# Thirty-one matrix products without a reader, placed on TensorE ahead of the first transposes and ahead of the first projection of a four-layer perceiver block

## The chip, the cores and the metric

The kernel runs on one core of one Trainium2 chip. The metric is device time in microseconds (us) of that core. Beside the times there is one profiled execution, from which all rows below are taken; its time axis begins at the first instruction. TensorE is called PE in the rows (PEld is its weight load), VectorE DVE, ScalarE ACT, GpSimd POOL, and SPq is the queue from which the loads are issued.

## What is computed

Two sequences of 256 tokens with 256 features go through a layer normalisation and then four layers of self-attention, cross-attention over a context with a lookback mask, and a gated feed-forward part. After that come one windowed attention layer and one feed-forward layer with quantised weights. Only the very beginning matters here:

```python
x = x + _L0_xattn_ref(_layernorm(x, axis=-1), ctx_1024, itok_BxS_0_255, ...)
# in _L0_xattn_ref, four times:
h = rmsnorm(x, n1[l])
qkv = h @ Wqkv[l].T + bqkv[l]
q, k, v = jnp.split(qkv, 3, axis=-1)
q = apply_rope(split_heads(q, H), cos, sin)
k = apply_rope(split_heads(k, H), cos, sin)
```

## The kernel before

The program is written engine by engine: each engine has its own list of calls, in an order written out by hand, and counted semaphores tie the lists together. A token block b (0 or 1) has 256 tokens in two tiles of 128. An engine carries out its list strictly in order, so an instruction that waits holds up everything behind it on that engine.

The start of the program is one chain through four engines. SyncE's queue issues the loads one after the other: the input `X0` of both blocks, then `const` (an identity matrix, causal mask, rotary tables), then the norm weights, the first weights, and the rest. VectorE takes the mean and variance of block 0, GpSimd makes the inverse roots (`lrs`, `rstd`), and VectorE writes the normalised rows `hs`. TensorE turns them with four transposes against the identity in `const` (`norm_T(0, 0, 0)`, line 320). VectorE copies the result out of PSUM and weights it, into `hT` (line 1744, `weigh_T`). TensorE then projects them to queries and keys (`queries_keys(0, 0, 0)` and `(0, 0, 1)`, line 326: for each token tile two products of 128x128 weights by 512 columns, in float32). VectorE adds the bias on the way out of PSUM (`HID`, line 1752, `biased_qk`), and rotates (`AQ`, lines 1770 to 1791), and TensorE transposes the rotated rows (`rotated_T`, line 359), and so on.

On VectorE the copy to `hT` of block 0 stands ahead of the second half of block 1's normalisation (`X`, line 1936, and `hs`, line 1735), and that stands ahead of the first `HID`.

TensorE writes small results to four PSUM banks in turn. A dictionary `uses` numbers the uses in the order in which TensorE's list makes them. Use n writes bank n modulo 4 and waits until the use four before it was emptied; `filled` and `emptied` give the other engines the count to wait for:

```python
def next_bank(l, use):
    uses[l, use] = len(uses)
def bank(l, use):
    return psD[uses[l, use] % DBANKS]
def free_for(l, use):
    return free(l, use), uses[l, use] // DBANKS + 1
```

VectorE counts all four banks as free once before its first work. `pool_set` is counted by GpSimd when it has written `ones`, a 128x128 float32 tile. TensorE's list begins with a wait for `c_ld`, the landing of `const`.

Of the kernel before, what the change touches and what calls it, by code (L numbers as in the profile page):

```python
# [14 lines left out]
P = 128  # L15
# [62 lines left out]
def perceiver(nc, x_in, ctx_in, seg_in, wa_in, wb_in, wc_in, nrm_in, bias_in, vec_in, wt_in, wf_in, const_in, out):  # L78
    stack = ExitStack()
    with stack:  # L80
        def sb(name, shape, dt=F32):
            return stack.enter_context(nc.sbuf_tensor(name, shape, dt))
# [4 lines left out]
        def sem(name):  # L87
            return stack.enter_context(nc.semaphore(name))
# [83 lines left out]
        ones = sb("ones", [P, P])  # L172
# [48 lines left out]
        pool_set, tern_step = sem("pool_set"), sem("tern_step")  # L221
# [27 lines left out]
# [6 lines that stand above are left out]
        def full(l, use):  # L255
            return d_full[uses[l, use] % DBANKS]

        def free(l, use):
            return d_free[uses[l, use] % DBANKS]
# [4 lines left out]
        def free_for(l, use):  # L264

            return free(l, use), uses[l, use] // DBANKS + 1

        def emptied(l, use):
            return free(l, use), uses[l, use] // DBANKS + 2
# [43 lines left out]
        def _(pe):  # L313
            def transposes(l, use, src):

                next_bank(l, use)
                pe.wait_ge(*free_for(l, use))
                for k in range(KT):
                    for t in range(QT):
                        mm = pe.transpose(bank(l, use)[:, k * L + t * P:k * L + (t + 1) * P],  # L320
                                          src[:, t, k * P:(k + 1) * P], ident)
                mm.then_inc(full(l, use), 1)

            def project(l, use, col, lhs, rhs, n=D):
                for k in range(KT):
                    mm = pe.matmul(bank(l, use)[:, col:col + n], lhs(k), rhs(k), start=(k == 0), stop=(k == KT - 1))  # L326
                return mm

            def norm_T(l, i, b):
                pe.wait_ge(h_set[b], l * NORMS + i + 1)  # L330
                transposes(l, f"n{i}{b}", hs[:, 2 * b:2 * b + 2, :])

            def queries_keys(l, b, t):
                pe.wait_ge(*emptied(l, f"n0{b}"))
                pe.wait_ge(wa_ld, l * 16 + 16)
                use = f"qk{b}{t}"
                next_bank(l, use)
                pe.wait_ge(*free_for(l, use))
                project(l, use, 0, lambda k: hT[b][:, k, t * P:(t + 1) * P], lambda k: Wqkv[:, k, 0:2 * D], 2 * D)\
                    .then_inc(full(l, use), 1)  # L340
# [400 lines left out]
            def quantised_down(t):  # L741
# [6 lines left out]
                                   WQ[2][:, f * D:(f + 1) * D], start=(f == 0), stop=(f == FT - 1))  # L748
                mm.then_inc(full(NL, f"d{t}"), 1)

            def sums():

                next_bank(NL, "sum")
                pe.wait_ge(asum_set, 3 * ABS_CHUNKS)
                pe.wait_ge(pool_set, 1)
                pe.wait_ge(*free_for(NL, "sum"))
                pe.matmul(bank(NL, "sum")[:, 0:3 * ABS_CHUNKS], ones[:, :], asum[:, :], start=True, stop=True)\
                  .then_inc(full(NL, "sum"), 1)
# [119 lines left out]
                pv(l + 1, 2)  # L878
            pe.wait_ge(c_ld, 16)

            norm_T(0, 0, 0)
            queries_keys(0, 0, 0)
            queries_keys(0, 0, 1)
            norm_T(0, 0, 1)
# [73 lines left out]
            def rest(further):  # L958
# [137 lines left out]
                if further:  # L1096
                    all_blocks(NL - 1, 1)
                sums()
                gate_up(NL - 1, 0, 5)
                out_T(NL - 1, 1, "coT1", 9)  # L1100
# [1659 lines left out]
```

## Time and profile before

| | |
|---|---|
| three timed runs | 622.4, 620.0, 622.28 us (median 622.28) |
| profiled execution, its own time | 619.67 us |
| span of that execution in the trace | 617.9 us |
| TensorE busy (product spans) | 564.1 us, 91% of the span |
| VectorE busy | 353.5 us, 57% |
| mean granted TensorE clock in the records | 0.991 |

The profiled execution's time is 1.8 us more than its span, for what lies around the first and last instruction. A busy TensorE in these rows is not TensorE at its peak: the spans of products overlap, since the next one begins before the last has left the array. A float32 product stands in the records as two weight loads and two passes, a transpose as one of each.

### The profile page before, as it was taken

The numbers are of one execution on the slowest core, as the hardware profiler recorded it, in microseconds if no ns is written. First come the engines' busy times: TensorE is split into PE (matmuls) and PEld (weight loads), VectorE is DVE, ScalarE is ACT, GpSimd is POOL, SyncE is SP. The second block draws the span as 40 slices with busy tenths as digits, with TensorE's granted clock in tenths as the row PEclk, the third lists the DMA queues.
The fourth block names the chain that finished last, engine by engine and source line by source line (L and its number), as shares of the span: only waits on it lengthen the run. The fifth ranks groups of instructions, "written<-read, shape, count | busy, mean of one in ns | idle before, by whom it ended". The sixth has DMA issues, their size and how long they took to land.

```text
span 617.9 us, 13676 instructions
## 1 busy us (share of the span) xinstructions
PE 564.1 (91%) x5806; PEld 421.8 (68%) x5806; DVE 353.5 (57%) x680; ACT 279.5 (45%) x490; POOL 117.7 (19%) x124
## 2 busy tenths in 40 slices
PE   4989998999999899999998989999898989999855
PEld 1666655988767566988766658987666558897523
DVE  5896445466564454674554455574554364752787
ACT  0254444633355336433544446342554547445523
POOL 4252100012323100020612000122312001252110
PEclk9999999999999999999999999999999999999969
DMA  8800020010500200201400200204000200000001
GB/s 334 345 2 25 12 69 2 5 65 1 205 2 4 102 1 3 68 1 27 180 1 36 70 2 2 69 1 189 16 2 1 71 0 2 0 1 2 2 1 39
DMA packets 4676, 30.29 MB, mean 49 GB/s; under 512 B 1153, under 2 KB 1665, under 8 KB 2818
## 3 DMA queue, kind: packets, MB, share of 16 engines
q1 hardware_dynamic: 4610, 29.35, 12.5%
q8 instruction: 49, 0.80, 0.5%
q14 instruction: 17, 0.14, 0.1%
HBM read 28.82 MB, written 0.52 MB: 47 GB/s over the span
## 4 chain that ended last, share of the span: by engine, by line
PE 77%; DVE 10%; ACT 8%; issue 3%; POOL 1%; DMA 1%; SPq 0%; DVEq 0%; POOLq 0%
PE psD L326 18%; PE QD L621 12%; PE psD L634 9%; PE QD L408 6%; PE QD L443 4%; ACT PTR L1253 3%; PE psD L320 3%; PE QD L436 3%; PE QD L394 3%; DVE AQ L1803 3%; PE psD L463 2%; PE QD L431 2%; PE psD L359 2%; PE psD L484 2%; PE psD L470 2%
## 5 line engine op out<-in xcount | busy, mean ns | idle before, releaser
L1253 ACT ACTIVATE PTR<-QD 128x2048 f32<-128x2048 f32 x40 | 75.1, 1878 | 41.8 <-PE QD L443 21.5
L326 PE MATMUL psD<-WAB,hT 128*128 128x256 f32 (+1 forms) x216 | 70.1, 465 | 2.2 <-DVE hT L1744 2.2
L2492 POOL TENSOR_TENSOR rstd<-ms,mhalf 128x2 f32<-128x2 f32 x26 | 19.9, 764 | 271.8 <-DVE ms L1729 270.6
L1803 DVE TENSOR_REDUCE AQ<-QD 128x8 f32<-128x2048 f32 (+1 forms) x24 | 55.0, 2290 | 27.0 <-PE QD L408 27.0
L621 PE MATMUL QD<-HH,WFH 128*128 128x256 f32 x224 | 67.4, 301 | 0.4 <-DVE WFL L1903 0.4
L1903 DVE TENSOR_TENSOR WFL<-WC,WFH 128x512 fp32r<-128x512 f32 x64 | 48.0, 755 | 32.2 <-ACT WFH L1297 32.1
L621 PE MATMUL QD<-HL,WFH 128*128 128x256 f32 x224 | 63.3, 283 | 0.0
L621 PE MATMUL QD<-HH,WFL 128*128 128x256 f32 x224 | 63.3, 283 | 0.0
L1800 DVE TENSOR_REDUCE AQ<-QD 128x16 f32<-128x2048 f32 x16 | 36.7, 2293 | 39.9 <-PE QD L408 39.9
L634 PE MATMUL psD<-WC,HID 128*128 128x256 f32 x256 | 58.2, 380 | 0.0
L326 PEld LDWEIGHTS psD<-WAB,hT 128*128 128x128 f32 x216 | 39.7, 195 | 21.0 <-issue 14.2
L1297 ACT ACTIVATE WFH<-WC 128x512 fp32r<-128x512 f32 x64 | 40.2, 629 | 26.0 <-PE QD L621 25.4
L634 PEld LDWEIGHTS psD<-WC,HID 128*128 128x128 f32 x256 | 47.4, 190 | 6.8 <-issue 1.0
L2534 POOL TENSOR_SCALAR_AFFINE_SELECT PTR<-PTR 128x1024 f32<-128x1024 f32 (+1 forms) x24 | 34.4, 1434 | 90.4 <-ACT PTR L1253 90.4
L408 PE MATMUL QD<-AQ 32*128 32x128 f32 (+1 forms) x1024 | 46.5, 312 | 0.0
L1261 ACT ACTIVATE QO<-psD 128x512 f32<-128x512 f32 (+1 forms) x40 | 20.5, 511 | 56.2 <-PE psD L470 40.6
L1222 ACT ACTIVATE hs<-X 128x256 f32<-128x256 f32 x48 | 19.5, 408 | 57.2 <-DVE X L1833 57.2
L621 PEld LDWEIGHTS QD<-HH,WFH 128*128 128x128 f32 x224 | 42.8, 191 | 3.2 <-issue 2.0
L408 PEld LDWEIGHTS QD<-AQ 32*128 32x128 f32 x1024 | 35.1, 185 | 13.9 <-issue 13.5
L621 PEld LDWEIGHTS QD<-HH,WFL 128*128 128x128 f32 x224 | 42.9, 191 | 0.9 <-issue 0.7
L621 PEld LDWEIGHTS QD<-HL,WFH 128*128 128x128 f32 x224 | 42.8, 191 | 0.0
L1833 DVE TENSOR_TENSOR X<-X,psD 128x512 f32<-128x512 f32 x24 | 16.5, 688 | 40.3 <-PE psD L326 29.5
(172 smaller groups left out, 1021.2 us busy)
## 6 DMA issues: line engine op xcount, KB each, us to landing
WC<-in_wc SPq DMA_DIRECT2D x4, 3072.0 KB, 10.9
WAB<-in_wa SPq DMA_DIRECT2D x4, 1024.0 KB, 4.9
WAB<-in_wb SPq DMA_DIRECT2D x4, 1024.0 KB, 4.7
WF<-in_wf SPq DMA_DIRECT2D x1, 3072.0 KB, 22.8
bias<-in_bias SPq DMA_DIRECT2D x4, 512.0 KB, 3.4
WAB<-in_wt SPq DMA_DIRECT2D x1, 1024.0 KB, 6.0
X<-in_x SPq DMA_DIRECT2D x2, 256.0 KB, 2.8
out_x<-X SPq DMA_DIRECT2D x4, 128.0 KB, 2.4
```

Source lines behind the costliest of these rows:

```text
L326: mm = pe.matmul(bank(l, use)[:, col:col + n], lhs(k), rhs(k), start=(k == 0), stop=(k == KT - 1))
L408: mm = pe.matmul(quad[a][:, at:at + keys], QKT[b][rows(a), s, q * P:(q + 1) * P], QKT[b][rows(a), s, L:L + keys], start=False, stop=True, ...
L443: mm = pe.matmul(quad[a][:, at:at + P], QKT[b][rows(a), s, L + k * P:L + (k + 1) * P], Q2[rows(a), n * P:(n + 1) * P], start=(at == 0), st ...
L621: mm = pe.matmul(S[:, w * L:(w + 1) * L], wp[:, m, :], hp[:, k, :], start=(k == 0 and j == 0), stop=(k == KT - 1 and j == 2))
L634: mm = pe.matmul(bank(l, use)[:, t * D:(t + 1) * D], AT[b][:, f, t * P:(t + 1) * P], Wd[:, f, :], start=(f == 0 and t == 0), stop=(f == FT ...
L1253: nc.scalar.activation(PTR[:, r % 2, :], QD[:, :], ACT.Exp, scale=SCALE).then_inc(t_exp, 1)
L1261: nc.scalar.activation(OA[:, 0:n], bank(l, use)[:, 0:n], ACT.Copy).then_inc(free(l, use), 1)
L1297: nc.scalar.activation(w_high(n), WCt[:, :, f * P:(f + 1) * P], ACT.Copy).then_inc(wh_set, 1)
L1800: v = dve.tensor_reduce(QKR[b][:, :, 0, h, MAXROW].rearrange("p t (s r) -> p r s t", r=SG_H), QD[:, :].rearrange("p (r s t n) -> p r s t n ...
L1803: v = dve.tensor_reduce(QKR[b][:, t, 0, h, MAXROW].rearrange("p (s r) -> p r s", r=SG_H), QD[:, :].rearrange("p (r s n) -> p r s n", r=4, ...
L1903: dve.tensor_tensor(w_low(n), WCt[:, :, f * P:(f + 1) * P], w_high(n), ALU.subtract).then_inc(wl_set, 1)
L2534: nc.gpsimd.affine_select(T, T, [[0, 16 // (t + 1)], [1, P]], ALU.is_ge, 0.0, base=0, channel_multiplier=-1)\
```

## The change

A new function `unread_products` takes a PSUM bank for itself, writes n products of `ones` by `ones` (128x128 by 128 columns, float32) to it, and counts the bank as filled after the first and as emptied after the last. It stands on TensorE's list at two places: 27 products behind the wait for `const` and a new wait for `pool_set`, ahead of `norm_T(0, 0, 0)`; and 4 products behind these transposes, ahead of `queries_keys(0, 0, 0)`. Since `uses` numbers all uses, every later small result moves to another of the four banks, on all engines alike.

```diff
+            def unread_products(use, n):
+
+                next_bank(0, use)
+                pe.wait_ge(*free_for(0, use))
+                for i in range(n):
+                    mm = pe.matmul(bank(0, use)[:, 0:P], ones[:, :], ones[:, :], start=True, stop=True)
+                    if i == 0:
+                        mm.then_inc(full(0, use), 1)
+                mm.then_inc(free(0, use), 1)
...
             pe.wait_ge(c_ld, 16)
 
+            pe.wait_ge(pool_set, 1)
+            unread_products("idle0", 27)
             norm_T(0, 0, 0)
+            unread_products("idle1", 4)
             queries_keys(0, 0, 0)
             queries_keys(0, 0, 1)
             norm_T(0, 0, 1)
```

This is TensorE's list of instructions at the start of the program, with + where the changed kernel has a row that the kernel before has not, and - for the reverse (L756 are the new products, L320 the transposes of `hs`, L326 the projections, each row with its number of products; float32 products count once here).

```order
 L312 UNCONDITIONAL_BRANCH
-L320 MATMUL psD<-const,hs 128x128 x4
+L756 MATMUL psD<-ones 128x128 x27
+L320 MATMUL psD<-const,hs 128x128 x4
+L756 MATMUL psD<-ones 128x128 x4
 L326 MATMUL psD<-WAB,hT 128x512 x4
 L320 MATMUL psD<-const,hs 128x128 x4
```

Nothing else moved: the transposes are the same four, now behind 27 products, and the first projection is behind 4 more.

The next rows are the head of the same list in the changed kernel, with the semaphores that each row waits for.

```order
0 L312 UNCONDITIONAL_BRANCH [waits barrier_Pool_Activation_PE_DVE_SP_release]
1 L756 MATMUL psD<-ones 128x128 [waits d_free0,pool_set,c_ld]
2 L756 MATMUL psD<-ones 128x128 x26
3 L320 MATMUL psD<-const,hs 128x128 [waits d_free1,h_set0]
4 L320 MATMUL psD<-const,hs 128x128 x3
5 L756 MATMUL psD<-ones 128x128 [waits d_free2]
6 L756 MATMUL psD<-ones 128x128 x3
7 L326 MATMUL psD<-WAB,hT 128x512 [waits d_free3,wa_ld,d_free1]
```

The wait for `const` (`c_ld`), which stood on the first transpose, is now on the first of the 27 products; the transposes wait for `hs` (`h_set0`) and the projection for `hT` (`d_free1`) as before.

## Rows read from the trace of the kernel before

**Rows 1.** The page: busy time and share; busy tenths in 40 slices.
```profile
PE 564.1 (91%) x5806; PEld 421.8 (68%) x5806; DVE 353.5 (57%) x680; ACT 279.5 (45%) x490; POOL 117.7 (19%) x124
PEclk9999999999999999999999999999999999999969
```

**Rows 2.** Waits of PE, 0 to 30 us: in total, times, longest (us).
```profile
PE psD L320 <- DVE hs L1735: 8.1, 1, 8.1
PE psD L326 <- DVE hT L1744: 1.0, 1, 1.0
```

**Rows 3.** Timeline, all engines, to 8 us: start, busy us, instruction, idle before.
```profile
0.95 0.20 POOL L2487 MEMSET ones<- 128x128 f32 x1
...
5.74 0.20 ACT L1308 ACTIVATE warm<-mhalf 128x1 f32<-128x1 f32 x1 [3.22 <-DMA const<-in_const]
5.78 0.72 POOL L2497 TENSOR_TENSOR lrs<-lve,mhalf 128x2 f32<-128x2 f32 x1 [1.70 <-DMA const<-in_const]
...
7.42 0.62 DVE L1735 TENSOR_SCALAR hs<-X,rstd 128x256 f32<-128x256 f32 x2
```

**Rows 4.** Timeline of PE, 8 to 24 us.
```profile
8.13 1.08 PE L320 MATMUL psD<-const,hs 128*128 128x128 f32 x4 [8.13 <-DVE hs L1735]
10.26 6.66 PE L326 MATMUL psD<-WAB,hT 128*128 128x512 f32 x8 [1.04 <-DVE hT L1744]
16.75 0.60 PE L320 MATMUL psD<-const,hs 128*128 128x128 f32 x4
17.36 1.09 PE L359 MATMUL psD<-const,AQ 128*128 128x128 f32 x8
...
20.19 1.17 PE L408 MATMUL QD<-AQ 32*128 32x128 f32 x32
...
21.79 1.88 PE L326 MATMUL psD<-WAB,hT 128*128 128x512 f32 x4
```

**Rows 5.** Timeline of PEld, 12 to 17 us: the weight loads of the passes.
```profile
12.13 0.34 PEld L326 LDWEIGHTS psD<-WAB,hT 128*128 128x128 f32 x1 [0.52 <-issue]
12.98 0.34 PEld L326 LDWEIGHTS psD<-WAB,hT 128*128 128x128 f32 x1 [0.52 <-issue]
...
15.54 0.34 PEld L326 LDWEIGHTS psD<-WAB,hT 128*128 128x128 f32 x1 [0.52 <-issue]
16.33 0.14 PEld L320 LDWEIGHTS psD<-const,hs 128*128 128x128 f32 x1 [0.45 <-issue]
```

**Rows 6.** Weight loads by form: busy us, mean ns of one.
```profile
L634 PEld LDWEIGHTS psD<-WC,HID 128*128 128x128 f32 x256 | 47.4, 190 | 6.8 <-issue 1.0
```

**Rows 7.** Timeline of DVE, 9 to 24 us.
```profile
9.33 0.88 DVE L1744 TENSOR_SCALAR hT<-psD,nrm 128x256 f32<-128x256 f32 x2
...
11.65 0.61 DVE L1735 TENSOR_SCALAR hs<-X,rstd 128x256 f32<-128x256 f32 x2
14.15 0.69 DVE L1752 TENSOR_TENSOR HID<-psD,bias 128x512 f32<-128x512 f32 x1 [1.89 <-PE psD L326]
...
16.61 0.69 DVE L1791 TENSOR_TENSOR AQ<-AQ,HID 128x512 f32<-128x512 f32 x1 [0.17 <-DVE HID L1780]
...
23.78 0.69 DVE L1752 TENSOR_TENSOR HID<-psD,bias 128x512 f32<-128x512 f32 x1
```

**Rows 8.** Windows near the end: busy us of each engine, then granted clock.
```profile
602.00:603.00 1.00, 1.00 (x3) 0.25 (x2) 0.61 (x1) 0.49 (x1) 0.00 (x0) 0.50 0.00 0
603.00:604.00 1.00, 1.00 (x5) 0.34 (x3) 0.64 (x1) 1.00 (x2) 0.00 (x0) 0.83 0.00 0
```

**Rows 9.** Timeline of PE near the end.
```profile
599.70 5.58 PE L728 MATMUL QD<-WAB,QO 128*128 128x512 bf16 x16 [0.68 <-issue]
```

**Rows 10.** Windows, 20 to 50 us: busy us of PE, PEld, DVE, ACT, POOL.
```profile
20.00:25.00 5.00, 5.00 (x58) 3.43 (x60) 4.15 (x5) 0.60 (x1) 0.45 (x1) 1.00 1.08 461
...
30.00:40.00 10.00, 8.98 (x140) 6.50 (x142) 9.60 (x18) 5.56 (x7) 4.90 (x4) 1.00 0.00 0
40.00:50.00 10.00, 9.04 (x161) 6.27 (x157) 9.22 (x20) 3.46 (x5) 3.04 (x3) 1.00 0.01 3
```

**Rows 11.** The chain of work that ended last, at its start: start, us, what.
```profile
1.73 3.99 DMA const<-in_const
5.78 0.72 POOL lrs L2497
...
10.26 6.66 PE psD L326 x8
16.92 0.44 PE psD L320 x4
17.36 0.67 PE psD L359 x4
```

## The prediction, made before the changed kernel ran

> **What bounds the kernel now.** I read the page first: TensorE is busy for 91% of the span [rows 1], so time given to it can only be free where it waits. Then the waits of TensorE in the first 30 us: it waits 8.1 us for the first rows `hs` and 1.0 us for `hT` [rows 2]. These two holes are the ones that the 31 products are put into. The question is when the products can start, how long they last, and whether they buy a faster clock.
>
> The timeline says when the holes are open. GpSimd has written `ones` at 0.95 + 0.20 = 1.15 us, but `const` has only landed when ScalarE and GpSimd, both waiting for it, go on at 5.74 and 5.78 us [rows 3]. TensorE's first instruction waits for `const` in both kernels. So the first hole is usable from about 5.75 us, not from 1.15, and it closes when `hs` is written: 7.42 + 0.62 = 8.04 us [rows 3], with the first transpose at 8.13 [rows 4]. That is 2.3 us of cover.
>
> The same rows show two speeds of TensorE. Passes of 512 columns follow each other by 12.98 - 12.13 = 0.85 us from 12 us on [rows 5], while the same form takes 1.88 / 4 = 0.47 us each at 21.79 [rows 4]. Four transposes took 1.08 us at 8.13 and 0.60 us at 16.75 [rows 4]. The page's slices write 9 there [rows 1], but the durations are those of half the clock, 1.2 against 2.4 GHz: the record shows no step before the first change of the clock. A weight load at 15.54 still takes the slow 0.34 us; the one at 16.33 the fast 0.14 [rows 5] (another form, but beside transposes that are fast). So full speed came between 15.9 and 16.3 us, about 5.6 to 6.1 us after the dense work began at 10.26.
>
> What waits for the slow stretch? VectorE starts on the first projected tile at 14.15, having idled 1.89 us for it [rows 7]. Behind it come the rotation and TensorE's next transposes at 17.36 [rows 4]; the chain that ended last runs through these very steps, beginning with the landing of `const` [rows 11]. The second projected tile is waited for by nobody: VectorE is on the first one's rotation until 16.61 + 0.69 = 17.30 [rows 7]. So of the slow clock only that part costs which delays 14.15.
>
> **The change, part by part.** *Length of the 27 products.* No float32 product of 128 columns on the full array that is not a transpose stands in the trace. Each is two passes: 54 passes. A pass of 512 columns costs 0.85 us at the slow clock [rows 5], so one of 128 costs 0.213. At the fast clock the columns give half, 0.107; eight transposes in a row take 1.09 us, and with 0.28 us for the last one's own length (what 0.60 for four leaves if the other three go at 0.107) the other seven go at 0.115 [rows 4]. The tiled products agree: 32 passes of 128 columns, four side by side, take 1.17 us, so eight sets at (1.17 - 0.28) / 7.75 = 0.115 [rows 4]. I take 0.213 slow and 0.115 fast. The upper bound is the full length of one weight load, 0.34 us slow [rows 5] and 0.19 fast [rows 6], if loads could not overlap each other. The tiled products, whose loads are as wide, speak against that.
>
> *When the clock rises.* The products are dense, so they should bring it. The two rises in this trace came 5.6 to 6.1 us after dense work began [rows 4, 5], and near the end, where the clock is 0.50 to 603.00 and 0.83 in the next us, so up at 603.33, 3.6 us after products began at 599.70 [rows 8, 9]. Between 3.6 and 6.1 us, middle 4.85: from 5.75 that is 9.35 to 11.85, middle 10.6 us.
>
> *The sum.* Slow until 10.6: 4.85 / 0.213 = 23 passes. The other 31 at 0.115 take 3.6 us, so the 27 products are through at 14.2 us, where the cover ended at 8.13. Transposes 0.60; 9.33 - (8.13 + 1.08) = 0.12 to VectorE; its copy 0.88; 10.26 - (9.33 + 0.88) = 0.05 back [rows 4, 7]: projection at 15.85. The 4 products of the second place, 8 x 0.115 = 0.9 us, start when the transposes have been issued, about 14.65, and end at 15.6: hidden under VectorE's copy. At the fast clock the first tile's four passes reach VectorE 23.78 - 21.79 = 1.99 us after their start [rows 4, 7], so `HID` begins at 17.85 instead of 14.15. The other input to that moment is VectorE's own list: block 1's `hs` ended 12.26 - 10.21 = 2.05 us after `hT` [rows 7], which gives 15.8 + 2.05 = 17.85 too. So a still faster projection would give no more. The step is **+3.7 us**.
>
> The price of the delay is 6.1 us (14.2 - 8.13), the gain of the clock is 0.5 us in the transposes and 3.89 - 1.99 = 1.9 us in the first tile.
>
> *Behind it.* VectorE has 9.60 of 10 us busy from 30 to 40 and 9.22 from 40 to 50, TensorE 5.00 of 5 from 20 to 25 [rows 10]. There is no slack there to take the 3.7 us up, and no load that both wait for. TensorE was fast from 16.3 us on already, so nothing later gains. The four banks are taken in the same order by all engines; the shifted count makes the second projected tile wait for the 27 products' own bank, long emptied, so I cost it at nothing. The waits for `pool_set` (1.15 us) and for the free banks are hidden by the wait for `const`; without that cover they would cost nothing either.
>
> Against its own execution the sum gives 619.67 + 3.7 = 623.4; against the median of the three runs, which lies 2.6 us higher, 622.28 + 3.7 = **626.0 us**. The forecast's own range: clock at 9.35 and the passes as above gives +2.8 (17 slow, 37 fast: through at 13.3); clock at 11.85 and 0.136 a fast pass (1.09 / 8, [rows 4]) gives +4.7. With about 1 us for what medians of such runs scatter, 624.1 to 628.0.
>
> A rule of the Trainium skill speaks to the length of a pass: TensorE: Matmul & The Clock Gate, section on the back-to-back issue gap, has columns streamed at one per cycle, start to start N / 1.2 ns slow and N / 2.4 + 2.5 ns fast. By it, and two passes a product, the estimate is 5.75 to 10.6 us at 0.107 = 45 passes, 9 more at 0.056, through at 11.1 us, +0.6 us in all. This trace's float32 passes take 0.85 us for 512 columns at the slow clock, two cycles per column, so I go by the row.
>
> **The rivals.** *Loads bind (0.10).* The passes go at the length of a weight load. Slow 4.85 / 0.34 = 14 passes, 40 at 0.19 = 7.6: through at 18.2 us, +7.7, 630.0 us. For it: no row has this very form. Against: the tiled products. If besides the clock did not rise on such products, 54 x 0.213 = 11.5 us, through at 17.3, and the first tile slow too: +8.7, 631; I keep that in the same 0.10.
>
> *One cycle per column (0.06).* Passes of `ones` go at half of what the projection's did: 54 passes with 45 before the clock rises, through at 11.1: +0.6, 622.9 us. Against: the rows of the same type. The rule above is this one.
>
> *The delay is taken up (0.12).* The step is 3.7 us at 17 us but layer 0's masks, counts and cross-attention, off VectorE's and ScalarE's list, close up again. For it: ScalarE and GpSimd are half idle from 30 to 50 [rows 10]. Against: VectorE is not. Half taken up is +1.8, 624.1 us.
>
> *Other side: the products fit (0.06).* The mechanism is that they are over when `hs` arrives and the clock is up by then or soon after. Place: from 5.75 to 8.13 us. Price: at best 0.5 us in the transposes and 1.9 in the first tile, -2.4, so 619.9 us. It decides if 54 passes take under 2.4 us, 0.044 us each, against 0.107 for the fast clock, or if the wait for `const` is over near 1.2 us, so that 6.9 us are covered. The chain begins with that landing [rows 11], so I give it little. Even this is -0.4%.
>
> **How the numbers follow.** Forecast 0.66. About 0.5% (3.1 us) is what a measurement of this kernel can tell from no change. Of the forecast's 0.66, where +3.1 is inside the range 2.8 to 4.7 and medians scatter by a us, I count 0.51 as slower and 0.15 as same; the 0.10 are slower; of the 0.12 and 0.06 nearly all is same, with 0.02 slower; of the last 0.06, 0.03 each to faster and same. Sum: slower 0.63, same 0.34, faster 0.03. The range takes in the forecast, half of taking-up and one cycle per column, and most of the way to loads that bind: 622.8 to 629.6.
>
> **What would show it.** In the changed kernel's timeline of TensorE: a first row of 54 passes at about 5.75 us (at 1.2, the wait is not what I think), 7.5 to 9.5 us long (over 11: loads bind; under 6: one cycle per column); a weight load that shortens from slow to fast between 9.3 and 11.9; transposes at 14.2 taking 0.6 us; `HID` on VectorE at 17.85, at 17 to 19 us in any case; then `AQ` and `rotated_T` later by the same step, and the same step still there at 60 us and at the end. A step that is there at 20 us but gone at 60 would be the taking-up.

## The result, and the profile after

| | before | changed |
|---|---|---|
| median of 8 runs each | 621.49 us (619.43 to 622.4) | 624.38 us (623.08 to 625.95) |
| ratio | | 1.0054, 95% interval 1.0037 to 1.0071 |
| profiled execution, its own time | 619.67 us | 623.08 us |
| its span | 617.9 us | 621.3 us |
| `HID` on VectorE begins | 14.15 us | 17.39 us |

By the ratio the change makes the kernel 0.54% slower, with 2.3 to 4.4 us inside the interval; the medians lie 2.9 us apart, and the profiled pair 3.4 us.

These are the waits of TensorE in the first 30 us of the changed kernel, to be read beside [rows 2]:

```profile
PE psD L756 <- DMA const<-in_const: 5.8, 1, 5.8
PE psD L359 <- DVE AQ L1804: 1.2, 1, 1.2
PE QD L398 <- ACT AQ L1242: 0.8, 1, 0.8
```

The waits for `hs` and `hT` are gone, and that is no gain: TensorE now waits for `const` first; the first product of `ones` does not read it but stands behind that wait. The hole that it was meant to fill lies mostly inside this wait. The 1.2 us for `AQ` are new; they come because the projection is now done before VectorE has rotated.

The timeline of all engines, changed kernel, beside [rows 3, 4, 7]:

```profile
5.77 0.20 ACT L1321 ACTIVATE warm<-mhalf 128x1 f32<-128x1 f32 x1 [3.25 <-DMA const<-in_const]
...
5.79 8.03 PE L756 MATMUL psD<-ones 128*128 128x128 f32 x54 [5.79 <-DMA const<-in_const]
...
7.42 0.62 DVE L1748 TENSOR_SCALAR hs<-X,rstd 128x256 f32<-128x256 f32 x2
...
13.66 0.60 PE L320 MATMUL psD<-const,hs 128*128 128x128 f32 x4
...
14.10 1.06 PE L756 MATMUL psD<-ones 128*128 128x128 f32 x8
14.37 0.88 DVE L1757 TENSOR_SCALAR hT<-psD,nrm 128x256 f32<-128x256 f32 x2 [5.18 <-PE psD L320]
...
15.30 3.70 PE L326 MATMUL psD<-WAB,hT 128*128 128x512 f32 x8
...
16.69 0.62 DVE L1748 TENSOR_SCALAR hs<-X,rstd 128x256 f32<-128x256 f32 x2
...
17.39 0.69 DVE L1765 TENSOR_TENSOR HID<-psD,bias 128x512 f32<-128x512 f32 x1
```

`hs` ends at 8.04 us in both kernels. The transposes come at 13.66 in place of 8.13, 5.5 us late, and VectorE idles 5.18 us for them. The faster clock gives back 0.5 us in the transposes (0.60 for 1.08) and, through the projection (3.70 us for its eight passes where it was 6.66), the rest up to VectorE's floor: `hs` of block 1 ends at 17.31, and `HID` follows at 17.39 with no idle time before it.

Where the clock rose is read from stretches of TensorE's timeline. These rows are what it shows of the 54 passes in five windows: at 8.8 us, from 7.5 to 9.3, at 9.37, at 10.05 and from 10.2 to 13.4 us.

```profile
8.51 0.63 PE L756 MATMUL psD<-ones 128*128 128x128 f32 x2
7.23 2.34 PE L756 MATMUL psD<-ones 128*128 128x128 f32 x10
9.15 0.54 PE L756 MATMUL psD<-ones 128*128 128x128 f32 x2
9.86 0.39 PE L756 MATMUL psD<-ones 128*128 128x128 f32 x2
9.97 3.62 PE L756 MATMUL psD<-ones 128*128 128x128 f32 x31
```

Two slow passes one behind the other take 0.63 us and ten take 2.34, so each further one adds 0.213 us. Behind the rise two take 0.39 and 31 take 3.62, which is 0.1115 us for each further one. The pair that starts at 9.15 lies between, with 0.54: the clock rose while its second pass ran, between 9.4 and 9.5 us, 3.7 us after the first pass. In this stretch the clock column of the profile says 1.00 before the rise too, so at the start of a trace it tells nothing; the durations do.

The delay then stays to the end. These are a row of VectorE in layer 0 and its last one, changed kernel:

```profile
60.52 2.28 DVE L1816 TENSOR_REDUCE AQ<-QD 128x8 f32<-128x2048 f32 x1
...
617.96 0.48 DVE L2054 SCALAR_TENSOR_TENSOR X<-psD,sgu,X 128x256 f32<-128x256 f32 x1 [0.39 <-PE psD L747]
```

and these are the same two before:

```profile
57.26 2.28 DVE L1803 TENSOR_REDUCE AQ<-QD 128x8 f32<-128x2048 f32 x1
...
614.69 0.48 DVE L2041 SCALAR_TENSOR_TENSOR X<-psD,sgu,X 128x256 f32<-128x256 f32 x1 [0.39 <-PE psD L747]
```

17.39 - 14.15 = 3.24 us at the first `HID`, 3.26 at 57 us and 3.27 at the last row. Nothing in 600 us of this pair takes up any of it.

### The profile page after: what moved, and what is told of

The parts are those of the page before. It is cut to its first block, busy times and chain, and to the rows that moved or that the text cites. A ratio compares the mean times of both kernels' runs of the same rounds, so it can differ in the third digit from the quotient of the medians.

```text
span 621.3 us, 13801 instructions
## 1 busy us (share of the span) xinstructions
PE 569.4 (92%) x5868; PEld 429.2 (69%) x5868; DVE 353.6 (57%) x680; ACT 279.5 (45%) x490; POOL 117.9 (19%) x124
## 4 chain that ended last, share of the span: by engine, by line
PE 76%; DVE 11%; ACT 8%; issue 3%; DMA 1%; POOL 1%; SPq 0%; DVEq 0%; POOLq 0%
PE psD L326 17%; PE QD L621 12%; PE psD L634 9%; PE QD L408 6%; PE QD L443 4%; ACT PTR L1266 3%; PE QD L436 3%; PE QD L394 3%; PE psD L320 3%; DVE AQ L1816 3%; PE psD L463 2%; PE QD L431 2%; PE psD L359 2%; PE psD L484 2%; PE psD L470 2%
## 5 line engine op out<-in xcount | busy, mean ns | idle before, releaser
L326 PE MATMUL psD<-WAB,hT 128*128 128x256 f32 (+1 forms) x216 | 67.1, 450 | 1.3 <-DVE hT L1757 1.2
L326 PEld LDWEIGHTS psD<-WAB,hT 128*128 128x128 f32 x216 | 38.6, 190 | 18.2 <-issue 12.6
## 6 DMA issues: line engine op xcount, KB each, us to landing
WC<-in_wc SPq DMA_DIRECT2D x4, 3072.0 KB, 10.3
WF<-in_wf SPq DMA_DIRECT2D x1, 3072.0 KB, 23.3
```

## The experiments

In what follows two things vary between executions without any edit: the moment at which `const` lands (what waits for it goes on at 5.60 to 7.18 us in the traces) and the moment at which the clock rises. So `HID` is told from the end of the products' row or from the end of `hs`, not from zero.

### More products, and one place at a time

Twice the products in the first place:

```diff
-            unread_products("idle0", 27)
+            unread_products("idle0", 54)
```

> 54 products in the first place in place of 27. My theory: the delay is the length of the passes, and those that are added all run at the fast clock. 54 more passes at 0.107 to 0.115 us are 5.8 to 6.2 us, so HID on VectorE begins at 23.2 to 23.6 us where the changed kernel has it at 17.39, and the end is later by the same step. Rival, weight loads bind at their own length (0.19 us fast): 10.3 us more, HID at 27.7. Rival, the 3.25 us come from something that the change does once (the second place, the shifted banks): HID stays near 17.4.

Only the first place:

```diff
             unread_products("idle0", 27)
             norm_T(0, 0, 0)
-            unread_products("idle1", 4)
```

> Only the 27 products of the first place, without the 4 of the second. My theory: the 4 lie under VectorE's copy to hT, so nothing changes: HID at 17.39 within 0.1 us. Rival, the 4 hold the projection up or keep the clock: HID moves by 0.3 us or more, or the passes of the projection go back to 0.85 us.

Only the second:

```diff
-            unread_products("idle0", 27)
             norm_T(0, 0, 0)
             unread_products("idle1", 4)
```

> Only the 4 products of the second place. My theory: at the slow clock they are 8 passes of 0.213 = 1.7 us behind transposes that are issued by about 9.0, so they outlast the copy and the projection begins near 10.75 instead of 10.26; its four first passes are slow as before: HID at 14.6, +0.5 us. If the clock rises during these passes, because the work is dense from 8.1 on, HID is at 13.5 to 14.2. Rival, the change's cost sits here: HID near 17.4.

One timed execution each: 630.26, 624.4 and 621.03 us; single times of this kernel scatter by about 3 us, so the readings rest on the traces. With 54 products the timeline shows

```profile
7.18 13.91 PE L756 MATMUL psD<-ones 128*128 128x128 f32 x108 [7.18 <-DMA const<-in_const]
...
24.66 0.69 DVE L1765 TENSOR_TENSOR HID<-psD,bias 128x512 f32<-128x512 f32 x1
```

`const` landed 1.4 us later in this execution, which is why `HID` is at 24.66 and not at 23.3. The length is what was asked: 13.91 - 8.03 = 5.88 us for 54 more passes, 0.109 us each. (In a fast stretch each is 0.1115 us, 6.0 us for 54; the clock rose 0.3 us sooner after the first pass than in the changed kernel, which gives back 0.15.) Loads that bind at 0.19 would have made it 10.3. The delay is the passes' length, at the fast clock for all but the first ones.

Without the second place:

```profile
6.00 8.63 PE L756 MATMUL psD<-ones 128*128 128x128 f32 x54 [6.00 <-DMA const<-in_const]
...
16.11 3.70 PE L326 MATMUL psD<-WAB,hT 128*128 128x512 f32 x8 [1.04 <-DVE hT L1756]
...
18.20 0.69 DVE L1764 TENSOR_TENSOR HID<-psD,bias 128x512 f32<-128x512 f32 x1
```

`HID` is not at 17.39, but the products started 0.21 us later and lasted 0.60 longer, because the clock rose 4.9 us after the first pass in place of 3.7. From their end it is 18.20 - 14.63 = 3.57 us, and 17.39 - 13.82 = 3.57 in the changed kernel. The projection is as fast behind a hole of 1.04 us as behind 4 products. So the second place does nothing there.

The second place alone:

```profile
8.42 1.09 PE L320 MATMUL psD<-const,hs 128*128 128x128 f32 x4 [8.42 <-DVE hs L1747]
...
9.30 1.91 PE L756 MATMUL psD<-ones 128*128 128x128 f32 x8
...
11.01 5.27 PE L326 MATMUL psD<-WAB,hT 128*128 128x512 f32 x8
...
14.68 0.69 DVE L1764 TENSOR_TENSOR HID<-psD,bias 128x512 f32<-128x512 f32 x1 [2.12 <-PE psD L326]
```

At the slow clock the 4 products outlast VectorE's copy (9.62 + 0.88 = 10.50) by half a us, and `HID` comes 6.5 us after the end of `hs` (8.16) where it was 6.1 before: +0.4, where +0.5 was expected. The shift of the banks costs nothing that can be seen: here it is by one bank, and in the kernels below that have both places, as the changed one does, by two.

### The same products, earlier

```diff
-            pe.wait_ge(c_ld, 16)
-
             pe.wait_ge(pool_set, 1)
             unread_products("idle0", 27)
+            pe.wait_ge(c_ld, 16)
             norm_T(0, 0, 0)
```

> The same 27 products, but ahead of the wait for const instead of behind it. My theory: the place of that wait is what makes them late. They start at about 1.2 us; the clock rises 3.6 to 6.1 us later, at 4.8 to 7.3; with 6.05, 23 slow passes and 31 fast ones at 0.11: through at 9.5 us, the transposes 1.4 us late, and HID at about 13.3 (12.9 to 13.9), 0.3 to 1.2 us earlier than in the kernel before; time 0.9 us below it, which a measurement does not tell from no change. Rival, the products delay for another reason than their start: HID still near 17.4.

619.06 us, median of 10 (618.48 to 619.71); ratio to the kernel before 0.9967, interval 0.9952 to 0.9981. Its timeline:

```profile
1.21 8.14 PE L756 MATMUL psD<-ones 128*128 128x128 f32 x54 [1.21 <-POOL ones L2499]
...
7.91 0.62 DVE L1747 TENSOR_SCALAR hs<-X,rstd 128x256 f32<-128x256 f32 x2
9.18 0.60 PE L320 MATMUL psD<-const,hs 128*128 128x128 f32 x4
...
12.92 0.69 DVE L1764 TENSOR_TENSOR HID<-psD,bias 128x512 f32<-128x512 f32 x1
```

The row is as long as in the changed kernel (8.14 against 8.03) and starts at 1.21 in place of 5.79. `HID` again follows its end by 12.92 - 9.35 = 3.57 us. The same 31 products make the kernel slower or faster, by where one wait stands. In the trace the gain is 1.2 us at `HID`, the upper end of what was expected, and 1.06 us in the execution's time; by the medians it is 2.25 us, where 0.9 was expected. The traced execution before, 619.67 us, lies 1.6 us below its kernel's median in this set, and this one 0.45 us below; that is the difference.

19 products there, sized to end before `hs`:

```diff
-            unread_products("idle0", 27)
+            unread_products("idle0", 19)
```

> 19 products ahead of the wait for const, 4 in the second place. My theory: 38 passes from 1.2 us, 23 to 26 slow ones and the rest at 0.11, are through by 7.7 to 8.2 us, so they fit under the wait for hs, which goes on to 8.0 us or later, and the fast clock is there for the transposes and the projection. HID then comes 3.8 us after the end of hs, the floor that VectorE's own list sets (6.11 in the kernel before, 4.39 with 27 products ahead, 9.35 in the changed kernel). Time 2.3 us below the kernel before, -0.4% (0.3 to 0.5). Rival, the clock has fallen again or rises only after the transposes: HID 5 to 6 us after hs, time within 1 us of the kernel before. Rival, the gain of 27 ahead was not from the clock: no more than -0.33% here.

> The same kernel as 19 ahead, run again beside the next two. Expected: the start as before (HID 4.1 us or less after the end of hs), time 0.3 to 0.5% below the kernel before. If the clock's fall in mid-kernel that its trace showed at 505 us comes and goes between executions, single times scatter by up to 2 us and the trace shows it elsewhere or not at all; if the fall follows from the products, it is at 505 us again.

618.35 us, median of 6 (617.73 to 619.49), ratio 0.9959 (0.9944 to 0.9975); in the second set 618.84, median of 12 (617.58 to 620.01), ratio 0.9977 (0.9966 to 0.9989). So it is faster than the kernel before, by 0.41% in the first set and by 0.23% in the second, where 0.3 to 0.5% was expected. The first set's trace:

```profile
1.20 7.15 PE L756 MATMUL psD<-ones 128*128 128x128 f32 x38 [1.20 <-POOL ones L2499]
...
7.46 0.62 DVE L1747 TENSOR_SCALAR hs<-X,rstd 128x256 f32<-128x256 f32 x2
8.19 0.61 PE L320 MATMUL psD<-const,hs 128*128 128x128 f32 x4
...
12.16 0.69 DVE L1764 TENSOR_TENSOR HID<-psD,bias 128x512 f32<-128x512 f32 x1
```

`HID` 12.16 - 8.08 = 4.1 us after `hs`, 2.0 us earlier than before. VectorE's rows keep these 2.0 us until 505 us, where `HL` begins at 505.31 for 507.21 before; the next one, `WFL`, begins at 513.79 for 514.12, and 1.6 of the 1.9 us left are gone. The windows of this kernel there (last three numbers: clock, DMA share, GB/s):

```profile
502.00:504.00 2.00, 1.01 (x8) 0.54 (x6) 1.27 (x4) 2.00 (x2) 0.47 (x1) 1.00 0.00 0
504.00:506.00 2.00, 1.14 (x4) 0.37 (x4) 1.93 (x4) 0.81 (x3) 0.00 (x0) 0.78 0.00 0
506.00:508.00 2.00, 2.00 (x18) 1.22 (x16) 0.01 (x1) 0.00 (x0) 0.00 (x0) 0.50 0.00 0
```

The granted clock falls to half at 505.1 us, behind 3 us in which TensorE was busy for less than half. The kernel before has the same work there without a fall in its one trace. The second trace of 19 ahead has no such fall: its VectorE rows are still 1.74 us ahead at 543 us. The fall is not a consequence of the products, since the kernel without any, whose GpSimd wait alone was moved (below), shows it too.

### A few products inside the cover

```diff
-            unread_products("idle0", 27)
+            unread_products("idle0", 5)
             norm_T(0, 0, 0)
-            unread_products("idle1", 4)
+            unread_products("idle1", 2)
```

> The changed kernel with 5 and 2 products in place of 27 and 4, all behind the wait for const. My theory: what costs is only the length that outlasts the cover. 10 slow passes are 2.1 us, through at 7.9, before hs; 4 slow passes are 0.85 us and end with VectorE's copy. So nothing is late, and since the work is dense from 5.8 us on, the clock rises 3.6 to 6.1 us later, 9.4 to 11.9, for part of the projection: HID 4.2 to 6.1 us after the end of hs, time 0 to 1.9 us below the kernel before (0 to -0.3%). Rival, the first place costs whatever its length, through the shifted banks or the new waits: HID 7 us or more after hs.

620.07 us, median of 12 (617.89 to 621.45); ratio 0.9988, interval 0.9975 to 1.0. The trace:

```profile
5.84 2.50 PE L756 MATMUL psD<-ones 128*128 128x128 f32 x10 [5.84 <-DMA const<-in_const]
...
8.14 1.05 PE L320 MATMUL psD<-const,hs 128*128 128x128 f32 x4
...
10.23 3.70 PE L326 MATMUL psD<-WAB,hT 128*128 128x512 f32 x8 [0.60 <-DVE hT L1757]
...
12.32 0.69 DVE L1765 TENSOR_TENSOR HID<-psD,bias 128x512 f32<-128x512 f32 x1
```

All behind the same wait for `const`, but within the cover: no delay, and in this execution (617.89 us, the fastest of the twelve) the clock rose before the projection, 3.2 us after the first product: the transposes at 8.14 are slow, and the four passes at 9.03 take 0.61 us, fast ones. The others reach up to 621.45; that the clock rises later in those would explain it, but their traces were not taken.

### GpSimd's wait for `const`

```diff
             pads()
 
-            pool.wait_ge(c_ld, 16)
             ln_rsqrt(0)
             rsqrt(0, 0, 0)
             ln_rsqrt(1)
             rsqrt(0, 0, 1)
+            pool.wait_ge(c_ld, 16)
```

With the 19 products ahead, and alone on the kernel before:

> As 19 ahead, and GpSimd waits for const only after its four inverse roots, which do not read it. My theory: const lands at 5.8 to 7.2 us from one execution to the next, and hs follows it only through this wait on GpSimd. Without it hs ends at 7.6 us whenever const landed, TensorE waits for const and hs together, and HID is 3.8 us after hs still, at 11.4: 0.4 to 1.5 us earlier than 19 ahead alone. The products end at 7.7 to 8.2, so they may now be 0.1 to 0.6 us late and take part of that back. Time -0.45 to -0.6% against the kernel before. Rival, GpSimd's wait is not what hs follows: hs ends where it did, no gain over 19 ahead.

> The kernel before with only GpSimd's wait for const moved behind its four inverse roots; no products. My theory: hs ends at 7.6 us in place of 8.0 or later, the clock is as before, HID 6.1 us after hs: 0.4 to 1 us less, -0.1%, not to be told from no change by the times, but plain in the trace. Rival: hs stays at 8.0 because another input is late.

Alone: 619.75 us, median of 12 (619.25 to 622.73), ratio 0.9988 (0.9974 to 1.0002). `hs` ends at 7.05 + 0.62 = 7.67 us as forecast, with `const` at 6.26; `HID` begins at 13.78, 0.37 us earlier than before. Its windows in mid-kernel:

```profile
504.00:506.00 2.00, 0.66 (x4) 0.42 (x4) 1.72 (x5) 2.00 (x4) 0.02 (x1) 1.00 0.00 0
506.00:508.00 2.00, 1.59 (x8) 0.51 (x8) 1.49 (x3) 0.36 (x1) 0.00 (x0) 0.71 0.00 0
508.00:510.00 2.00, 2.00 (x20) 1.20 (x24) 0.00 (x0) 0.00 (x0) 0.00 (x0) 0.50 0.00 0
```

With 19 ahead: 619.11 us, median of 12 (617.16 to 620.86), ratio 0.997 (0.9956 to 0.9985). This is not the gain that I expected (-0.45 to -0.6%). The start is right: `hs` ends at 7.66, the products are now the later ones, at 8.46, 0.8 us behind `hs` where 0.1 to 0.6 was expected, and `HID` is at 12.04, 2.1 us ahead of the kernel before. But then the rows of TensorE read

```profile
15.26 1.09 PE L359 MATMUL psD<-const,AQ 128*128 128x128 f32 x8 [1.18 <-DVE AQ L1803]
17.14 1.78 PE L398 MATMUL QD<-causB,identB 128*128 128x512 bf16 x4 [0.78 <-ACT AQ L1241]
18.84 2.02 PE L408 MATMUL QD<-AQ 32*128 32x128 f32 x32
```

and the windows

```profile
17.00:18.00 1.00, 0.86 (x3) 0.41 (x4) 0.83 (x5) 0.04 (x1) 0.21 (x1) 0.63 1.08 467
18.00:19.00 1.00, 1.00 (x7) 0.16 (x5) 0.58 (x1) 0.00 (x0) 0.00 (x0) 0.50 1.03 442
```

The clock fell to half at 17.3 us, behind two waits of 1.18 and 0.78 us, and 1.6 of the 2.1 us were gone at 21 us (32 tiled products in 2.02 us where they took 1.17 [rows 4]). The projection that is over early leaves TensorE a hole of 1.18 us in which the slow one had kept it busy. That this hole let the clock fall was my reading when I planned the next pair. The other traces speak against the hole as a sufficient cause: the changed kernel's, both of 19 ahead, that of 27 ahead and five more have the same two waits, of 1.17 and 0.78 or 0.79 us, and no fall there. These are the two rows with 16 products ahead (next section):

```profile
14.95 1.09 PE L359 MATMUL psD<-const,AQ 128*128 128x128 f32 x8 [1.17 <-DVE AQ L1803]
16.83 1.02 PE L398 MATMUL QD<-causB,identB 128*128 128x512 bf16 x4 [0.78 <-ACT AQ L1241]
```

### Shorter, and the hole filled

```diff
-            unread_products("idle0", 19)
+            unread_products("idle0", 16)
```

> 16 products ahead of the wait for const, and GpSimd's wait moved. My theory: 32 passes are through between 6.2 and 8.0 us, in most executions before hs at 7.66, so the transposes no longer wait for them; HID 3.8 us after hs, at 11.5 to 11.6, 2.6 us earlier than in the kernel before, time -0.4%. Rival: the shorter stretch leaves the clock slow in some executions, so that HID comes 5 to 6 us after hs.

and to that, for the second kernel,

```diff
             norm_T(0, 0, 1)
+            unread_products("idle2", 5)
             rotated_T(0, 0, 0, 1)
```

> As 16 ahead with GpSimd's wait moved, and 5 products more behind the transposes of block 1, in TensorE's wait of 1.2 us for AQ before rotated_T. The trace of 19 ahead with GpSimd's wait moved shows the clock fall at 17.4 us behind that hole and another of 0.8 us, and 1.6 us lost by it. My theory: a projection that is done early leaves more of TensorE idle between 14 and 17 us, and that lets the clock fall in some executions; filled, it stays up: no fall before 25 us, times 0 to 0.8 us below those of 16 ahead without the fill, and less scattered. Ten passes at 0.107 are 1.07 us and fit in the hole. Rival, the fall has nothing to do with the hole: the same median and scatter.

16 ahead: 618.37 us, median of 12 (616.93 to 619.47), ratio 0.9968 (0.9956 to 0.9979), where 0.4% less was expected. `HID` at 11.74, 4.1 us after `hs` (7.66), 2.4 us ahead of the kernel before. The 0.3 us over the expected 3.8 are VectorE's:

```profile
7.04 0.62 DVE L1747 TENSOR_SCALAR hs<-X,rstd 128x256 f32<-128x256 f32 x2
7.57 0.74 DVE L1938 BATCH_NORM_STATS2 bst<-X 128x6 f32<-128x256 f32 x2
...
8.63 0.17 DVE L1943 TENSOR_SCALAR lve<-mv 128x2 f32<-128x2 f32 x1
8.71 0.88 DVE L1756 TENSOR_SCALAR hT<-psD,nrm 128x256 f32<-128x256 f32 x2
```

Block 1's statistics stand between `hs` and `hT` on its list, with no idle time before `hT`: the transposes, over at 8.39, wait for VectorE. So `hT` cannot begin earlier than 1.05 us after `hs`, however fast TensorE is (19 ahead has 9.14 - 8.08 = 1.06).

Filled: 617.71 us, median of 6 (617.09 to 617.95), ratio 0.9956 (0.9939 to 0.9973), the fastest of all kernels tried. The 10 passes took 1.28 us, a little more than the hole, and cost 0.2 us behind `rotated_T`. Neither trace has a fall of the clock before 25 us, so the traces do not tell the two kernels apart in this. The medians differ by 0.7 us and the spread is smaller with the fill, as the theory has it, but the intervals of the ratios overlap and 6 runs are few. Whether the fill does anything, and why the clock fell in one execution and not in the others, stays open.

## Why the prediction was right

The forecast was 626.0 us, slower, with 622.8 to 629.6; measured 624.38. By its own steps:

- **The place of the wait.** Forecast: products from 5.75, not from 1.15. Measured 5.79, with `const` as the releaser. Shown to be the cause by moving it: 3.2 us slower at the first `HID` behind it, 1.2 us faster ahead of it.
- **The length of the 27 products.** Forecast 8.4 us, to 14.2; the transposes began at 13.66, 0.5 us earlier. That is the clock: it rose at about 9.5 and not at 10.6 us, which is worth 0.5 us. The fast pass is 0.1115 and not 0.115 us, 0.1 less in all, and the second pass starts 0.16 us later behind the first than slow passes do further on, which the forecast did not have. All of it lies inside the bounds given, but the rise is close to the early one (3.7 us for 3.6 to 6.1), and other traces have it 2.9 to 3.4 us after the first product: the bounds that I took from three rises were too narrow.
- **The price of a pass, two cycles per column.** 0.213 us for 128 columns at 1.2 GHz is 256 cycles; at 2.4 GHz these would be 0.107 us, and 0.1115 was measured. The rule of the Trainium skill on the back-to-back gap (TensorE: Matmul & The Clock Gate), one cycle per column, gave the prediction's estimate of 11.1 us for the end of the row, which came at 13.82. The trace does not agree with it for float32.
- **Weight loads don't bind.** 0.11 against 0.19 us a pass, by doubling the products and from the rows above.
- **The second place is hidden.** The products took 1.06 us from 14.10 and ended with VectorE's copy (15.25). Taking them away changed nothing.
- **VectorE's floor.** Forecast that block 1's `hs` and the first tile arrive together; `HID` has no idle time before it in the changed kernel. The step was +3.24 for a forecast of +3.7.
- **Nothing takes it up.** 3.24, 3.26, 3.27 us at 17, 60 and 618 us, in the one pair of traces. This rival is out.
- **From step to median.** 0.8 of the 1.6 us between forecast and measurement come from the baseline: the median before is 621.49 over 8 runs and was 622.28 over 3. 0.45 is the step. The rest is within the scatter.

Two sums of the prediction don't come out as written. With the clock up at 9.35 us and 37 passes at 0.115 the products are through at 13.6 us, +3.1; its 13.3 and +2.8 take 0.107 for a fast pass. And 54 slow passes, through at 17.3 us with no gain behind them, make +9.1 and not +8.7. Neither changes the forecast.

The rival of the other side, that the products fit, was priced at -2.4 us at best and held to decide only if the wait for `const` were over near 1.2 us. With that wait moved, 19 products give 2.0 us at `HID`. Most of the other 0.4 is a floor that I had overlooked, block 1's statistics ahead of `hT` on VectorE; it did not matter to the forecast, where `hT` came long after them.

## What to carry to other kernels

Before filling a wait with work, read what ends the wait first: a hole of 8 us in which the filler itself must wait 5.8 us is a hole of 2.3. Warm-up work belongs ahead of every wait that it doesn't need, sized so that its slow-clock length ends before the real input. What a faster clock can give at one place is bounded by the next engine's own list (2.0 us here, of a slow stretch 6 us long), while what outlasts the cover is paid in full, and in a kernel with no slack it is still there 600 us later.

## What the runs showed of the hardware

The clock rose 3.7 us after the first of a dense row of passes in the changed kernel. In the other rows it is worked out from their lengths: 0.16 us for the late second pass (the first two take 0.80 us where later slow pairs take 0.63) and 0.28 us for the last one's own length (0.39 - 0.11), then 0.213 or 0.1115 us for each pass but one. So 7.15 us for 38 passes has 25 to 26 of them slow, and the rise is 5.6 us after the first; 6.34 us for the same 38 in the second trace has 17 to 18, and 3.9 us. With 54 products it rose after 3.4 us, with the first place alone after 4.9, with 27 ahead after 3.9, with 19 ahead and GpSimd's wait moved after 5.8, with 16 ahead after 3.9 and, in the kernel with the fill, after 2.9. The same kernel thus has a different slow stretch each time; in the two traces of 19 ahead the row's length differs by 0.8 us for it.

The clock also fell in mid-kernel, in some executions and not in others with the same work: at 17.3 us behind the waits of 1.18 and 0.78 us, at 505 and 507 us in both cases behind 3 us in which TensorE was busy for less than half. Each cost 1.4 to 1.6 us, against the 2.0 us at `HID` that 19 products ahead gained. A gain at the start can be lost there in one execution and kept in the next. Near the end of the kernel it falls in all thirteen traces: the last two slices of the profile page's clock row read 69 before, 79 in the changed kernel, and 69, 78, 79 or 88 in the others.
